# Other engines and another order for the last rounding, the last normalisations, PE's opening products and the first keys

## The reference

```python
x = x + xattn(layernorm(x), ctx, ctx, mask, Wq, Wk, Wv, Wo)   # 16 heads of 8, causal mask
x = x + attn(layernorm(x), ...)                               # scores * decay, softmax
x = x + ffn(layernorm(x), w1, b1, w2, b2)

def quant_per_tensor(x):
    scale = max(max(abs(x)), 1e-6) / 127      # one scale for the whole tensor
    return round(x / scale), scale
def qlinear(x2d, w, b):
    xq, sx = quant_per_tensor(x2d); wq, sw = quant_per_tensor(w)
    return (xq @ wq.T + b) * (sw * sx)
ffn(x) = qlinear(gelu(qlinear(x, w1, b1)), w2, b2)
```

## Time and profile before

| | |
|---|---|
| median of 3 runs | 315.71 us (314.49 to 316.68) |
| the profiled execution | 315.6 us |
| its span, first to last instruction | 313.7 us |
| busy share of the span | PE 92%, DVE 81%, ACT 76%, POOL 74% |
| TensorE clock granted, mean | 0.977 of full speed |
| scores of the first tile start at | 9.19 us |
| scores of tiles 32 and 63 start at | 132.79 and 253.00 us |

### The profile page before, as it was taken

How to read it: one execution, slowest core, us unless ns; L and a number is a source line. 1 busy time by engine, 2 the same in 40 slices (tenths; PEclk the granted TensorE clock), 3 DMA queues, 4 the chain that set the end, 5 groups by cost and what they waited for, 6 DMA issues and landing times. The chain is left out here.

```text
span 313.7 us, 13645 instructions
## 1 busy us (share of the span) xinstructions
PE 288.6 (92%) x5744; PEld 198.1 (63%) x5744; DVE 255.1 (81%) x555; ACT 239.8 (76%) x529; POOL 232.2 (74%) x183
## 2 busy tenths in 40 slices
PE   7769979999999999999999999999999999699583
PEld 2347647676767767685768686867777777332273
DVE  2887779999888888887888787878788998579864
ACT  3584958585869898787888888898878877699580
POOL 5686849766888978799999999999899952430230
PEclk9998999999999999999999999999999999899869
DMA  7999000000000000000000000000000000000027
GB/s 232 309 276 288 9 2 4 2 2 5 4 2 2 4 2 3 5 2 2 4 2 5 3 4 2 5 3 5 2 2 4 2 5 5 0 0 2 0 67 203
DMA packets 16542, 11.64 MB, mean 37 GB/s; under 512 B 5153, under 2 KB 14690, under 8 KB 16482
## 3 DMA queue, kind: packets, MB, share of 16 engines
q1 hardware_dynamic: 15762, 10.34, 12.0%
q10 hardware_dynamic: 720, 0.43, 0.5%
HBM read 8.67 MB, written 2.10 MB: 34 GB/s over the span
## 5 line engine op out<-in xcount | busy, mean ns | idle before, releaser
L843 ACT ACTIVATE pt<-ps 128x512 f32<-128x512 f32 x128 | 75.9, 594 | 21.4 <-PE ps L591 20.6
L411 POOL TENSOR_TENSOR u<-u,mx 128x1024 f32<-128x1024 f32 x32 | 60.8, 1903 | 26.8 <-DVE mx L1059 26.6
L403 POOL TENSOR_TENSOR ud<-u,con 128x1024 f32<-128x1024 f32 x31 | 73.5, 2371 | 1.5 <-DVE u L1045 1.4
L1040 DVE SCALAR_TENSOR_TENSOR u<-ps,rs,arena 128x1024 f32<-128x1024 f32 x32 | 40.9, 1279 | 15.0 <-PE ps L572 13.3
L572 PE MATMUL ps<-arena,qT 32*64 32x256 f32 x1024 | 44.3, 402 | 6.4 <-ACT arena L836 4.0
L1045 DVE TENSOR_SCALAR u<-ps 128x1024 f32<-128x1024 f32 x32 | 39.0, 1219 | 12.5 <-PE ps L572 12.1
L618 PE MATMUL ps<-pt,vx 128*32 128x64 f32 x2048 | 41.4, 222 | 1.8 <-DVE oT L981 0.9
L618 PEld LDWEIGHTS ps<-pt,vx 128*32 128x32 f32 x2048 | 32.5, 111 | 15.5 <-issue 9.3
L624 PE MATMUL ps<-pt,con 128*32 128x128 f32 x1024 | 40.0, 275 | 0.0
L1059 DVE TENSOR_REDUCE mx<-u 128x16 f32<-128x1024 f32 x32 | 38.7, 1210 | 0.1
L572 PEld LDWEIGHTS ps<-arena,qT 32*64 32x64 f32 x1024 | 14.9, 129 | 32.7 <-issue 21.6
(11 more groups left out here) (153 smaller groups left out, 550.7 us busy)
## 6 DMA issues: line engine op xcount, KB each, us to landing
out<-pt SPq DMA_DIRECT2D x8, 256.0 KB, 3.0
arena<-in_ctx_cols SPq DMA_DIRECT2D x4, 256.0 KB, 4.5
xn3T<-in_x_cols SPq DMA_DIRECT2D x4, 256.0 KB, 4.7
x<-in_x SPq DMA_DIRECT2D x4, 256.0 KB, 5.2
arena<-in_ctx_cols SPq DMA_DIRECT2D x2, 512.0 KB, 5.8
xn3T<-in_x_cols SPq DMA_DIRECT2D x2, 512.0 KB, 5.3
x<-in_x SPq DMA_DIRECT2D x2, 512.0 KB, 8.6
arena<-in_mask_BxS_if SPq DMA_DIRECT2D x2, 256.0 KB, 6.7
```

Of the source, the lines that this page charges most:

```text
L403: pool.tensor_tensor(dh, uh, decay.unsqueeze(1).to_broadcast([P, H, HALF]), ALU.mult)\
L411: pool.tensor_tensor(uh, uh, mx[:, n % 4, 0:count].unsqueeze(2).to_broadcast([P, count, HALF]), ALU.subtract)\
L843: act.activation(pt[:, n % 2, 4 * half:4 * half + 4].rearrange("p h n -> p (h n)"), ps[:, bank, :], ACT.Exp).then_inc(s["emptied"], 1)
L1040: dve.scalar_tensor_tensor(by_head(u[:, n % UB]), sc, rs[:, 0, n:n + 1], mask[:, n].unsqueeze(1).to_broadcast([P, H, HALF]), ALU.mult, ALU ...
```

## The change

It edits five places.

- **Opening.** Values of group 1 go from turn 2 to turn 3, and the expansions of the keys of group 1 from turns 1, 2, 2, 3 to 1, 1, 2, 2. POOL makes the mask of tiles 8 to 31 in six pieces of four tiles (turns 4, 6, 9, 11, 13, 15) in place of three of eight tiles (turns 2, 5, 8).
- **Last normalisations.** `root` of tiles 24 to 27 goes from turn 66 to 65; `xn3` gets a third buffer; the transposes of group 4 go from turn 65 to 66; POOL keeps tile 28, and tiles 29 and 30 go from POOL to DVE; the maximum of group 6 goes ahead of DVE's last addition to x, and the maximum of group 7 is taken in one instruction.
- **Opening products.** `open_up(2)` and `open_up(3)` go from ahead of hidden pieces 0 and 1 to behind them, each just ahead of its own piece.
- **Last rounding.** POOL has no part in it. DVE rounds group 0 in halves, 3, 6 and the second half of 7; ACT rounds 1, 2, 4, 5 and the first half of 7.
- **Order of the down products.** PE, the evictions and the DMAs go through the groups as 0, 1, 3, 2, 6, 4, 5, 7, with DVE's roundings between its evictions.

```diff
-ROOT_TURN = (..., (46, 54, 62, 66, 67, 69))
+ROOT_TURN = (..., (46, 54, 62, 65, 67, 69))
-H_ACT, H_POOL = (1, 3, 5, 7), (2, 6)
-DVE_TAIL = (("a", 0), ("a", 4)) + tuple(("f", g) for g in range(8))
+DOWN = (0, 1, 3, 2, 6, 4, 5, 7)
+H_ACT = ((1, 0, 2), (2, 0, 2), (4, 0, 2), (5, 0, 2), (7, 0, 1))
+H_DVE = ((0, 0, 1), (0, 1, 2), (3, 0, 2), (6, 0, 2), (7, 1, 2))
...
-    early = ([("v", 0)], [("k", 1), ("q", 1)], [("v", 1)], [], [("k", 2)], [("q", 2)])
+    early = ([("v", 0)], [("k", 1), ("q", 1)], [], [("v", 1)], [("k", 2)], [("q", 2)])
...
-        pieces[APPLY3[g] + (2 if g < NG - 1 else 0)].append(("x3", g))
+        pieces[APPLY3[g] + (3 if g == 4 else 2 if g < NG - 1 else 0)].append(("x3", g))
...
-                pool.wait_ge(s["filled"], gets_empty(("x3", g - 2)))
-                pool.wait_ge(s["amax_done"], g - 1)
+                pool.wait_ge(s["filled"], gets_empty(("x3", g - 3)))
+                pool.wait_ge(s["amax_done"], g - 2)
...
-                    last_norm(7, range(28, 31))
+                    last_norm(7, range(28, 29))
...
-            pe.wait_ge(s["emptied"], max(fill.values()) + 1)
-            open_up(2)
-            pe.wait_ge(s["ascale"], 1)
-            open_up(3)
             for k in range(16):
                 pair, c = divmod(k, FC)
+                if k == 2:
+                    pe.wait_ge(s["emptied"], max(fill.values()) + 1)
+                    open_up(k)
+                if k == 3:
+                    pe.wait_ge(s["ascale"], 1)
+                    open_up(k)
...
-                        if n == (GT * j - EXPAND[j // NG][h] if j > 2 else ((1, 2, 2, 3), (5, 5, 6, 7))[j - 1][h]):
+                        if n == (GT * j - EXPAND[j // NG][h] if j > 2 else ((1, 1, 2, 2), (5, 5, 6, 7))[j - 1][h]):
...
-                if n == NS - 1 + LAG_ADD[1]:
+                if n == NS - 1 + LAG_PV[1]:
                     dve.wait_ge(s["xn3_pool"], 1)
                     largest(6, 0, GT, 6)
                 if n == APPLY3[7]:
+                    last_norm(7, range(29, 31))
                     last_norm(7, range(31, 32))
                     dve.wait_ge(s["xn3_pool"], 2)
-                    largest(7, 0, 3, 7)
-                    dve.wait_ge(s["xn3_last"], 2)
-                    largest(7, 3, 4, 8)
+                    dve.wait_ge(s["xn3_last"], 3)
+                    largest(7, 0, GT, 7)
```

More of the change, by code:

```diff
@@ L41 @@
          ((0, 8), (8, 8), (16, 8), (24, 4), (28, 3), (31, 1)))
-ROOT_TURN = ((-1, 1, 4, 7, 12, 17), tuple(15 + 4 * g for g in range(8)), (46, 54, 62, 66, 67, 69))
+ROOT_TURN = ((-1, 1, 4, 7, 12, 17), tuple(15 + 4 * g for g in range(8)), (46, 54, 62, 65, 67, 69))
 POOLED = 4
@@ L302, in _ @@
                 sp.dma_start(dst, src).then_inc(s["ffw_in"], 16)
[L303 to L305 removed]
+            for m, g in enumerate(DOWN):
+                sp.wait_ge(s["ob_ready"], m + 1)
+                sp.dma_start(out_t[:, g * GT:(g + 1) * GT], ob[:, (m % 4) * GT:(m % 4 + 1) * GT]).then_inc(STORED[m % 4], 16)
             for n in range(4):
@@ L548, in piece @@
                     for i in range(GT):
-                        if j == 7 and i == 3:
-                            pe.wait_ge(s["xn3_last"], 2)
-                        last = pe.transpose(ps[:, bank, i * P:(i + 1) * P], xn3[:, j % 2, i], ident)
+                        if j == 7 and i in (1, 3):
+                            pe.wait_ge(s["xn3_last"], 2 if i == 1 else 3)
+                        last = pe.transpose(ps[:, bank, i * P:(i + 1) * P], xn3[:, j % 3, i], ident)
                 last.then_inc(s["filled"], 1)
@@ L713, in _ @@
             open_down(5)
-            for g in range(NG):
-                if g == 1:
+            for m, g in enumerate(DOWN):
+                if m == 1:
                     open_down(6)
-                if g == 2:
+                if m == 2:
                     pe.wait_ge(s["hscale"], 1)
                     open_down(7)
-                if g in H_ACT:
-                    pe.wait_ge(s["hr_done"], H_ACT.index(g) + 1)
-                elif g in H_POOL:
-                    pe.wait_ge(s["hr_done_pool"], H_POOL.index(g) + 1)
-                else:
-                    pe.wait_ge(s["hr_done_dve"], 1 if g == 0 else 3)
-                for i in range(GT):
-                    if g == 0 and i == 2:
-                        pe.wait_ge(s["hr_done_dve"], 2)
+                for i in range(GT):
+                    for e, part in enumerate(H_ACT):
+                        if part[0] == g and i == 2 * part[1]:
+                            pe.wait_ge(s["hr_done"], e + 1)
+                    for e, part in enumerate(H_DVE):
+                        if part[0] == g and i == 2 * part[1]:
+                            pe.wait_ge(s["hr_done_dve"], e + 1)
                     for c in range(FC):
```

67 lines of the change are left out of this document (31 added, 36 removed).

## The result

The changed kernel takes 312.71 us (median of 8, 312.13 to 313.66), the kernel before 315.02 in the same comparison: a ratio of 0.992, interval 0.9895 to 0.9945. That is 0.8% where 2.1% was forecast, and 0.5 above the range. The span went from 313.7 to 311.6.

A forecast was written before the change was run, and what follows sets the result against it. PE was taken as the bound from 55 to 131 us, and a chain of waits near the end; gains of 2.7 + 1.4 + 0.3 + 2.2 = 6.6 off 315.6 gave 309.0 us, range 307.0 to 312.2.

The forecast's parts named there:

- If the clock therefore stays up, the turn lasts what turn 5 lasted: Opening, turn 4: at full clock it takes 4.68 less work already counted, so tile 5's scores come at about 25.3.
- the 2.7: Opening: gain taken from having group 1's keys expanded earlier, 2.9 less hand-offs; lower end 1.4.
- The third rival: Whole kernel: two or more terms lie beside something unseen, gaining 0 to 3.2, 312.4 to 315.6 us; chance 0.09.
- The second rival: Opening gives half or nothing, as the clock falls or a later wait takes it back: 310.3 to 311.7; chance 0.15.
- The value that was taken: Last normalisations: DVE beside POOL takes 0.37 against 0.28, costing at worst some 0.4 of the 1.4 gain.
- the 2.39 of the tail: Last rounding: DVE's second half beside POOL; evidence for mutual waiting in the last normalisations, 1.1 to 1.9 lost, chance 0.13.
- 1.6 by the slot: Last rounding: gain if the last eviction must wait for its output slot, free at 308.5 after a DMA of 3.94.
- the rival that would have made it slower: Mask pieces: POOL's late pieces hold up PE, up to 10.5 lost, 319.5 us with all of it; chance 0.03.
- the 2.9 taken as the most: Last rounding: upper bound of the gain, with neither low clock nor a long output DMA.
- the 6.6 forecast: Whole kernel: summed gain of opening 2.7, last normalisations 1.4, opening products 0.3 and last rounding 2.2.
- two places taken as fixed: Hidden maximum to first rounding, and last eviction to the end: both forecast to change by 0.

The follow-up runs named there:

- the three causes removed: The changed kernel with loads spread out, twelve more products in PE's idle time ahead of the second maximum, and output written in place into x: 308.96 us, ratio 0.9788.

## Why the prediction was wrong

**Opening: the step that failed is "If the clock therefore stays up, the turn lasts what turn 5 lasted".** All that it named came out: keys in time, scores of tile 4 at 21.40 (21.4 forecast), the clock at 1.00. What it did not count is that PE's instructions themselves come by DMA. With them in time the turn ends at 25.82 and 2.3 to 2.4 of the 2.7 are there (33.29 to 30.94). Without, two stops of 1.2 and 1.0 idle take all back: the turn lasts 5.69 instead of the 3.9 forecast, and turn 6 lasts 5.04 instead of the 3.79 of before. The load was in the trace of before as a line of section 3 with 1.0% of the DMA time, hidden behind the very wait that the change removed. Where the stall goes, something else is late next: this something was the code.
The Trainium skill (Runtime: NRT & Kernel Launch, section "Instruction fetch mechanics") describes code that is fetched in blocks of 16 KiB, 256 instructions, by a DMA queue of the engine, at a cost that is mostly hidden. The size and the spacing agree with the loads and stops here; "mostly hidden" holds in the profile after for all loads but the two of the opening, where data is loaded at the same time.

The third rival is the one that came: 312.71 lies in its 312.4 to 315.6, and two terms, the opening and the last rounding, lay beside something unseen. It had 0.09 and named no cause. The second rival had the opening's amount right (nothing) and its cause wrong: neither did the clock fall in turns 2 to 4, nor did the wait ahead of tile 8 take anything. Part of the 2.7 was also not certain to be there: turn 4 of the kernel before takes 5.36 to 5.41 in three of the profiled executions with the old opening and 3.80 in two, as the clock falls or not. Against the latter the opening's edit is worth 0.8 to 0.9 (31.73 and 31.87 to 30.94).

**Last normalisations: right,** 1.45 for 1.4. POOL beside DVE cost DVE nothing and POOL 0.24. The value that was taken, from the row of the same instruction, was the better one; by the 2.39 of the tail 1.1 to 1.9 should have gone.

**Opening products: right,** 0.4 for 0.3: the first product on x came 0.6 earlier, and 0.2 of that was lost again before the hidden maximum. The clock moves this stretch by more than the edit does: over all profiles it took 22.76 to 23.55 with the old order and 22.54 to 23.20 with the new.

**Second maximum: not in the prediction at all.** It took 1.76 as an unchanged part of the way. It takes 2.4 to 2.5 where the clock falls within 0.5 of its start, and 1.76 with the clock up. In the profile of before the fall came 0.2 before the stage's end, at 296.16; in that of after at 292.77, ahead of its first product. Without the new tail it happens as well. With products in PE's idle time it took 1.76 or 1.77 in five profiles of five; without them 2.39 to 2.49 in six of ten, 1.94 in one, and 1.76 or 1.77 in three (before, before with spread loads, and the 100 products at PE's start). That speaks for the products, though without them, too, it stayed under 2 in four of ten: part of the 0.7 is the luck of two single executions. Why the clock falls at the one place in one execution and later in another was not settled.

**Last rounding: the term was mis-sized,** 1.1 for 2.2. The mechanism was right: both halves in 1.42, the last eviction set by the slot. The size was taken between "1.6 by the slot" and 2.9, while in the profile after the slot decided, and with 4.3 rather than 3.94, since a load of PE's code stands beside the third and fourth output DMAs. The low clock over the first groups (295.12 to 299.60 at 0.50) counts only together with the slots: without slots the stretch took 10.64 at the same low clock, a gain of 3.1 and more than the 2.9 taken as the most; with slots and the clock up it took 10.34. Beyond it, the way from the last eviction to the end grew by 0.2, as the last output DMA took 2.53 instead of 2.29.

**Mask pieces: right,** nothing either way; the rival that would have made it slower didn't happen.

So of the 6.6 forecast, 2.6 are missing in the opening, 1.1 in the tail, and 0.9 were lost in two places taken as fixed (0.7 and 0.2); 2.1 is left in the span, with the 0.1 of the long stretch between. With the three causes removed the kernel takes 309.0, 2.1% less than before and 1.2% less than the change as made, which happens to be the forecast's number.

## What to carry to other kernels

When an edit takes a wait away, look at what was being fetched during that wait, code included: a queue of kind "instruction" in the DMA section, and idle time of PE put down to "issue" in the middle of equal instructions, are its signs. Loads that aren't needed yet are better issued later, when code has to pass the same DMAs. And a stage that is short because PE's clock is up is only as safe as the work ahead of it: a few products in an idle stretch are cheap, but pay only where no later wait lets the clock fall all the same.

## What the runs showed of the hardware

A load of code of 16 KB takes 0.9 to 1.6 us, and where PE stands still for it, it goes on 1.25 to 1.57 after its end (eleven stops in seven profiles, each in front of the 450th instruction or one a multiple of 256 behind it). One such load of 0.94 makes output DMAs of 256 KB that are under way take up to 4.3 instead of 2.3, more than its own length. With the same edit, the stretch from tile 0 to tile 8 took 32.6 to 33.2 us where code came late and 30.6 to 31.1 where the loads were spread or the borders of 256 instructions lay elsewhere. The granted clock fell at different places of the program in executions of the same part of it (in turn 4 of the old opening in three of five), so one profiled execution is no safe base for what a low clock costs.
